# A GNN block on one Trainium2 core: D to the columns of H B H^T by a row through DRAM and a GpSimd product, and another order within a step

## The reference, cut to what matters

```python
def hypergraph_conv(x, adj, W, b):
    H = (adj != 0).astype(x.dtype)
    w = adj.reshape(N, -1)[:, :C]                 # first row of adj
    xw = jnp.einsum('ncd,hd->nch', x, W)
    Dn = jnp.einsum('nce,ne->nc', H, w)
    Dn = jnp.where(Dn > 0, 1.0 / Dn, 0.0)
    Be = H.sum(axis=1)
    Be = jnp.where(Be > 0, 1.0 / Be, 0.0)
    m = Be[:, :, None] * jnp.einsum('nce,nch->neh', H, xw)
    return Dn[:, :, None] * jnp.einsum('nce,neh->nch', H, m) + b
h = layer_norm(relu(hypergraph_conv(x, adj, W1, b1)), gamma, beta)   # 256 -> 512
y = hypergraph_conv(h, adj, W2, b2) + x                             # 512 -> 256
out = _layernorm(x + y)
```

## Time and profile before

| | us |
|---|---|
| runs shown | 300.36, 301.17, 301.25 |
| median | 301.17 |
| the profiled execution | 300.86 |
| its span | 299.1 |
| busy in it: PE | 285.9 |
| DVE | 207.1 |
| ACT | 207.4 |
| POOL | 133.7 |
| q1, SP's queue: share of 16 DMA engines | 23.5% |

### The profile page before, as it was taken

One profiled execution on the slowest core, in us unless ns is written; L12 is line 12 of the kernel. 1 busy time (PEld: TensorE's weight loads), 2 busy tenths in 40 slices (PEclk: granted clock), 3 DMA queues, 4 the chain that ended last, 5 costly groups with the idle time before them and its releaser, 6 DMA issues.

```text
span 299.1 us, 5864 instructions
## 1 busy us (share of the span) xinstructions
PE 285.9 (96%) x1918; PEld 254.5 (85%) x1918; DVE 207.1 (69%) x589; ACT 207.4 (69%) x619; POOL 133.7 (45%) x162
## 2 busy tenths in 40 slices
PE   5799999999999999999999999999999999999972
PEld 5689889798988989898898979898897989988851
DVE  1783686794939587593958669494958759394965
ACT  3498577868687786868677786858778686756430
POOL 2233444617353552636344361735355263636441
PEclk9999999999999999999999999999999999999995
DMA  7921030503114050502305050310304040101112
GB/s 217 297 72 36 1 107 0 175 2 125 56 30 148 0 179 0 172 7 57 120 1 175 2 176 2 109 34 8 133 3 140 2 141 0 59 13 37 37 50 90
DMA packets 26437, 22.55 MB, mean 75 GB/s; under 512 B 860, under 2 KB 26152, under 8 KB 26408
## 3 DMA queue, kind: packets, MB, share of 16 engines
q1 hardware_dynamic: 26304, 22.15, 23.5%
q10 hardware_dynamic: 104, 0.04, 0.0%
HBM read 13.80 MB, written 8.39 MB: 74 GB/s over the span
## 4 chain that ended last, share of the span: by engine, by line
DVE 32%; POOL 27%; issue 23%; PE 11%; ACT 3%; DMA 2%; DVEq 0%; POOLq 0%; SPq 0%
POOL xb_sb L781 11%; DVE r_lo L595 7%; POOL rstd L774 7%; DVE g_sb L586 6%; DVE bn_sb L623 6%; DVE z_sb L615 6%; POOL rstd L796 5%; PE bank_v L253 4%; POOL r_hi L789 4%; DVE mv_sb L633 2%; DMA w_raw<-in_L_gnn_W_dram 2%; PE bank_v L238 1%; POOL shift L801 1%; DVE mean L636 1%; DVE u_lo L558 1%
## 5 line engine op out<-in xcount | busy, mean ns | idle before, releaser
L789 POOL TENSOR_SCALAR r_hi<-r_sb 128x512 fp32r<-128x512 f32 x64 | 48.2, 753 | 82.4 <-ACT r_sb L436 82.4
L261 PE MATMUL bank_g<-w_hi,r_hi 128*128 128x258 f32 x256 | 69.3, 303 | 0.0
L263 PE MATMUL bank_g<-w_lo,r_hi 128*128 128x256 f32 x256 | 63.8, 281 | 0.0
L436 ACT ACTIVATE r_sb<-bank_v,vec 128x512 f32<-128x512 f32 x64 | 44.2, 690 | 15.8 <-PE bank_v L253 15.8
L253 PE MATMUL bank_v<-u_hi,w_hi 128*128 128x512 f32 x128 | 51.9, 406 | 0.4 <-DVE u_lo L558 0.4
L253 PE MATMUL bank_v<-u_lo,w_hi 128*128 128x512 f32 x128 | 50.5, 395 | 0.0
L253 PE MATMUL bank_v<-u_hi,w_lo 128*128 128x512 f32 x128 | 50.4, 394 | 0.0
L263 PEld LDWEIGHTS bank_g<-w_lo,r_hi 128*128 128x128 f32 x256 | 48.4, 189 | 1.0
L261 PEld LDWEIGHTS bank_g<-w_hi,r_hi 128*128 128x128 f32 x256 | 48.3, 189 | 1.1
L595 DVE TENSOR_TENSOR r_lo<-r_sb,r_hi 128x512 fp32r<-128x512 f32 x64 | 47.6, 747 | 1.5 <-POOL r_hi L789 1.5
L268 PE MATMUL bank_g<-w_hi,r_lo 128*128 128x258 f32 x256 | 41.3, 283 | 0.0
(11 more groups left out here) (95 smaller groups left out, 485.2 us busy)
## 6 DMA issues: line engine op xcount, KB each, us to landing
x_sb<-in_x_dram SPq DMA_DIRECT2D x16, 512.0 KB, 3.8
out_dram<-z_sb SPq DMA_DIRECT2D x15, 512.0 KB, 4.6
adj_sb<-in_adj_dram SPq DMA_DIRECT2D x16, 256.0 KB, 5.0
w_raw<-in_L_gnn_W_dram SPq DMA_DIRECT2D x2, 512.0 KB, 6.2
out_dram<-z_sb SPq DMA_DIRECT2D x2, 256.0 KB, 2.2
b_half<-in_L_gnn_b_dram SPq DMA_DIRECT2D x1, 128.0 KB, 7.3
edge_rows<-in_adj_dram ACTq DMA_DIRECT2D x1, 32.0 KB, 3.2
vec_rows<-in_L_gnn_b_dram ACTq DMA_DIRECT2D x1, 2.0 KB
```

Of the source, the lines that this page charges most:

```text
L261: pe.matmul(bank_g[:, n, 0:W2COLS], r_hi[:, i % 2, k, graph(n)], w2_hi[:, k], start=(k == 0), stop=False)
L263: pe.matmul(bank_g[:, n, 0:DOUT], r_hi[:, i % 2, k, graph(n)], w2_lo[:, k], start=False, stop=False, skip_group_check=True)
L436: nc.scalar.activation(r_sb[:, k], bank_v[:, k % 2], ACT.Relu, bias=vec[:, k:k + 1]).then_inc(relu_ready, 1)
L789: nc.gpsimd.tensor_scalar(r_hi[:, i % 2, k], r_sb[:, k], 1.0, 1.0, ALU.mult, ALU.mult).then_inc(r_hi_ready, 1)
```

## The change

S is copied as it is from PSUM to s_sb by ScalarE (read_s), and the degrees with it. make_d works on that copy. SP stores dinv (128 x 4) to a DRAM tensor and loads it back as one row of 512, broadcast to all 128 partitions. GpSimd multiplies S by that row (make_at), which gives A^T. Groups 0 and 1 still go by make_a, turn_a and read_at. The order of a step changes on all engines: TensorE now has g 0, g 1, turn_q, make_u, make_s, g 2, v 0, g 3, v 1, v 2, v 3, y 0, y 1, turn_h(i+4). VectorE has add_squares(i) first, then z of group i-1 before split_u(i+1), make_d(i+2) behind it, then the statistics of z of group i-1, make_h, make_b, make_var1(i) and the rest. GpSimd adds b2 before it splits r, behind a wait for u_lo, and ends a step with make_at(i+2). make_htb(1) goes from ScalarE to GpSimd. The diff without its declarations:

```diff
@@ SP
+            def store_d(j):
+                sp.wait_ge(d_ready, j + 1)
+                sp.dma_start(d_rows[j], dinv[:, j % 2]).then_inc(d_stored, 16)
+
+            def load_d(j):
+                sp.wait_ge(d_stored, 16 * (j - ON_PE + 1))
+                if j >= ON_PE + 2:
+                    sp.wait_ge(at_ready, j - 1)
+                sp.dma_start(d_row[:, j % 2], d_rows[j].rearrange("c n -> (c n)").unsqueeze(0).to_broadcast(
+                    [P, P * PER])).then_inc(d_row_in[j % 2], 16)
             for i in range(G):
                 if i + 6 < G:
                     load_adj(i + 6)
+                if i + 2 < G:
+                    store_d(i + 2)
+                    load_d(i + 2)
                 if i + 3 < G:
                     load_x(i + 3)
-                if i >= 1:
-                    store(i - 1)
+                if i >= 2:
+                    store(i - 2)
@@ TensorE
             def make_s(j):
...
-                if j >= 2:
-                    pe.wait_ge(q_summed, j - 2)
-                else:
-                    pe.wait_ge(a_ready, j)
+                if j:
+                    pe.wait_ge(at_ready, min(j, ON_PE))
+                if j >= ON_PE:
+                    pe.wait_ge(q_summed, j - 1)
+                    if j + 1 < G:
+                        pe.wait_ge(ht_ready, j + 2)
             def turn_q(i):
                 pe.wait_ge(q_ready, i + 1)
-                pe.wait_ge(q_summed, i)
-                pe.wait_ge(a_ready, min(i + 3, G))
+                if i:
+                    pe.wait_ge(q_summed, i)
+                    pe.wait_ge(s_read, min(i, G - ON_PE))
+                else:
+                    pe.wait_ge(at_ready, ON_PE)
@@ TensorE, the loop over i
                 make_g(i, 0)
                 if i == 0:
-                    turn_h(2)
+                    turn_h(3)
+                    pe.wait_ge(c2_ready, 1)
+                make_g(i, 1)
+                if i:
+                    turn_q(i)
                 if not last:
                     make_u(i + 1)
-                if 0 < i and i + 2 < G:
+                if i and i + 2 < G:
                     make_s(i + 2)
+                make_g(i, 2)
                 if i == 0:
-                    pe.wait_ge(c2_ready, 1)
-                make_g(i, 1)
+                    turn_q(0)
+                if not last:
+                    make_v(i + 1, 0)
                 if i == 0:
                     make_s(2)
-                if last:
-                    turn_q(i)
-                else:
-                    make_v(i + 1, 0)
-                make_g(i, 2)
-                if not last:
-                    turn_q(i)
-                if i + 2 < G:
-                    turn_a(i + 2)
                 make_g(i, 3)
                 if last:
                     break
                 make_v(i + 1, 1)
-                if i + 3 < G:
-                    turn_h(i + 3)
                 make_v(i + 1, 2)
                 make_v(i + 1, 3)
                 make_y(i, 0)
                 make_y(i, 1)
+                if i + 4 < G:
+                    turn_h(i + 4)
@@ ScalarE
+            def read_s(j):
+                act.wait_ge(s_made, j + 1)
+                if j > ON_PE:
+                    act.wait_ge(at_ready, j)
+                nc.scalar.activation(s_sb[:, :, :].rearrange("p (b n) e -> p b (n e)", b=2),
+                                     bank_s[:, :, 0:2 * HCOLS], ACT.Copy).then_inc(s_read, 1)
+                if i:
                     sum_q(i)
+                split_u(i + 1)
+                if i == 0:
+                    sum_q(i)
+                if i and i + 2 < G:
+                    read_s(i + 2)
+                if i >= 2:
+                    normalise(i - 2, 0)
+                    normalise(i - 2, 1)
+                relu(i + 1, 0)
+                if i == 0:
+                    read_s(2)
+                for k in range(1, KH):
+                    square(i + 1, k - 1)
+                    relu(i + 1, k)
+                square(i + 1, KH - 1)
@@ VectorE
             def make_d(j):
-                degrees = s_parts[:, :, :, P]
-                dve.wait_ge(s_made, j + 1)
+                if j < ON_PE:
+                    degrees = s_parts[:, :, :, P]
+                    dve.wait_ge(s_made, j + 1)
+                else:
+                    degrees = s_sb[:, :, P]
+                    dve.wait_ge(s_read, j - ON_PE + 1)
...
-                nc.vector.scalar_tensor_tensor(out=dinv[:, :], in0=degrees, scalar=0.0, in1=degree[:, 1],
+                nc.vector.scalar_tensor_tensor(out=dinv[:, j % 2], in0=degrees, scalar=0.0, in1=degree[:, 1],
             for i in range(G):
+                add_squares(i)
+                if i:
+                    make_z(i - 1, 0)
+                    make_z(i - 1, 1)
                 if i < LAST:
                     split_u(i + 1)
                 if i + 2 < G:
                     make_d(i + 2)
-                if i < LAST:
-                    add_squares(i)
+                if i:
+                    take_stats2(i - 1, 0)
+                    take_stats2(i - 1, 1)
+                    make_var2(i - 1)
                 if i == LAST:
                     break
                 if i + 4 < G:
                     make_h(i + 4)
+                if i + 3 < G:
+                    make_b(i + 3)
                 make_var1(i)
                 split_r(i + 1, 0)
                 read_g(i)
                 split_r(i + 1, 1)
...
@@ GpSimd
+            def make_at(j):
+                pool.wait_ge(d_row_in[j % 2], 16 * (j // 2))
+                if j >= 3:
+                    pool.wait_ge(y_made, (j - 2) * 2)
+                nc.gpsimd.tensor_tensor(at_sb[:, j % 3], s_sb[:, :, 0:P],
+                                        d_row[:, j % 2].rearrange("p (c n) -> p n c", n=PER),
+                                        ALU.mult).then_inc(at_ready, 1)
...
+                pool.wait_ge(u_lo_ready, (i + 2) * KD)
+                add_b2(i)
+                split_r(i + 1, 0)
                 if i:
                     inverse_std2(i - 1)
-                if i == LAST:
-                    break
-                split_r(i + 1, 0)
-                add_b2(i)
                 inverse_std1(i)
-                split_r(i + 1, 1)
-                split_r(i + 1, 2)
-                split_r(i + 1, 3)
+                for k in range(1, KH):
+                    split_r(i + 1, k)
+                if i + 2 < G:
+                    make_at(i + 2)
```

More of the change, by code:

```diff
@@ L75, in hypergraph_block @@
         degree = sb("degree", [P, 2, PER])
-        dinv = sb("dinv", [P, PER])
+        dinv = sb("dinv", [P, 2, PER])
+        s_sb = sb("s_sb", [P, PER, HCOLS])
+        d_row = sb("d_row", [P, 2, P * PER])
         a_sb = sb("a_sb", [P, PER, P])
@@ L108, in hypergraph_block @@
         SUM = DOUT
+        d_rows = nc.dram_tensor("d_rows", [G, P, PER], F32, kind="Internal").ap()
+        ON_PE = 2
         weights_in = [sem(f"weights_in{n}") for n in range(4)]
@@ L189, in _ @@
                     load_adj(i + 6)
+                if i + 2 < G:
+                    store_d(i + 2)
+                    load_d(i + 2)
                 if i + 3 < G:
                     load_x(i + 3)
-                if i >= 1:
-                    store(i - 1)
+                if i >= 2:
+                    store(i - 2)
+            store(LAST - 1)
             for half in range(2):
@@ L202, in turn_h @@
                 pe.wait_ge(h_ready, j + 1)
-                if j:
-                    pe.wait_ge(at_ready, j)
+                if j == 1:
+                    pe.wait_ge(at_ready, 1)
+                elif j == 2:
+                    pe.wait_ge(a_ready, 2)
+                elif j == 3:
+                    pe.wait_ge(ht_ready, 3)
+                elif j:
+                    pe.wait_ge(s_read, j - 3)
                 for n in range(PER):
@@ L223, in turn_a @@
                 for n in range(PER):
-                    mm = pe.transpose(bank_h[:, graph(n)], a_sb[:, n], ident[:, :])
+                    mm = pe.transpose(turned_a[j][:, graph(n)], a_sb[:, n], ident[:, :])
                 mm.then_inc(a_turned, 1)
@@ L333, in _ @@
             sum_w2()
+            make_s(1)
             make_v(0, 2)
-            make_s(1)
             make_v(0, 3)
+            turn_a(1)
+            turn_h(2)
             make_c2()
-            turn_a(1)
             pe.wait_ge(w2_ready, 1)
@@ L416, in make_a @@
                     ins = nc.scalar.activation(a_sb[:, n], s_parts[:, n // 2, n % 2, 0:P], ACT.Copy,
-                                               scale=dinv[:, n:n + 1])
+                                               scale=dinv[:, j % 2, n:n + 1])
                 ins.then_inc(a_ready, 1)
@@ L482, in _ @@
             relu(0, 0)
-            make_htb(1)
             relu(0, 1)
+            make_a(1)
             act.wait_ge(w2_centred, 1)
@@ L487, in _ @@
             relu(0, 2)
-            make_a(1)
             relu(0, 3)
             read_at(1)
+            read_ht(2)
```

(15 more changed lines are left out.)

62 lines of the change are left out of this document (21 added, 41 removed).

## The result

The changed kernel takes 325.14 us (median of 4 runs, 324.12 to 325.55), against 300.76 (4 runs, 300.34 to 301.25) for the kernel before beside it: a ratio of 1.080, interval 1.0778 to 1.0821. It is slower, as forecast, but by 24.4 us where 12.5 were forecast, and above the range (298 to 321). The profiled span is 323.7 us.

The account below looks back on a forecast made before the run. TensorE, busy in 96% of the span, was taken as the bound. Thirteen steps of 18.1 instead of 17.14 us add 12.5, group 0 -0.6, group 14 +0.6: 300.86 becomes 313.4, as a median 313.7; range 298 to 321.

Parts of the forecast that it names:

- make_d's last instruction is held: VectorE: with both operands in SBUF, it waits from 3.9 to 5.8 us after make_u's start for GpSimd's b2 addition.
- first sums to GpSimd's rstd 0.91, rstd to g_sb 1.51: First norm on VectorE and GpSimd: these start-to-start times, read from the old profile, put g_sb at 10.8 after make_u's start.
- a product of 1.29: GpSimd's make_at, two inputs of 512 columns: 1.29 us, on a line between additions of 4 and 1024 columns.
- A: The forecast itself: both GpSimd collisions hold VectorE, the product going right behind r_hi(3): 313.7 us, chance 0.40.
- B: VectorE keeps the shared port through back-to-back instructions, so the product waits for the end of q: 307 us, chance 0.20.
- q and turn_q: End of VectorE's step: q ends at 17.4, z at 18.05, and make_u of the next group starts 0.05 later.
- The sum: Whole kernel: 13 steps add 12.5 us, group 0 gains 0.6, group 14 loses 0.6, tail 0, onto 300.86.
- TensorE's saving of 0.59 a step: TensorE without turn_a, one fp32 entry into g and turn_h's switch back: step 16.55 if it never waits, 0.59 less.
- turn_h's part: TensorE: turn_h read as 0.31 us; moved behind y, its four transposes alone are 0.20, so 0.11 is saved.
- The row through DRAM: SP's store of dinv and load of the row: taken as 2.2 + 2.7 us, in time, so nothing charged.
- rival D: The row lands 3 us after the product's place is free; product falls into sums or behind q: 307 to 314, chance 0.08.
- Rival E: Neither collision on VectorE, at make_d and r_lo(1), costs anything, so TensorE runs through: 292.7 us, chance 0.18.

Follow-up runs that it names:

- product cut: Changed kernel with b2's addition back at q, rstd2 ahead of r_hi(0), product on VectorE but only one column a graph computed from group 2 on: 296.77 us, 0.987.
- the last version: Changed kernel, b2's addition at q, product on VectorE, g 2 before turn_q, rstd2 and shift ending GpSimd's step, make_var1 before make_h and make_b: 295.67 us, 0.981.

## Why the prediction was wrong in size

The sign, the kind of mechanism and two of the places were right: TensorE gives up the bound, y waits for g_sb, and q is late behind the product. What failed first is which instruction of make_d is held. The step by the forecast's own points, for group 6 and for group 7, which stands for most:

| from U, us | forecast | group 6 | group 7 |
|---|---|---|---|
| stats begin | 5.7 | 6.24 | 6.21 |
| g_sb begins | 10.8 | 11.46 | 11.43 |
| y begins | 11.75 | 12.39 | 12.37 |
| r_lo(1) begins | 12.4 | 13.04 | 13.01 |
| pair sums begin | 15.5 | 14.84 | 16.18 |
| q has ended | 17.4 | 18.07 | 18.18 |
| next U | 18.1 | 18.82 | 18.93 |

- **"make_d's last instruction is held"** was the step that failed first. It is the first one, and the other two follow only after the addition: stats at 6.21, 0.51 late, 6.6 us over 13 steps and more than half of the miss. The forecast took the rule from rows of two-input instructions and applied it to the only such instruction in make_d. The runs show that a one-input fp32 tensor_scalar from SBUF to SBUF is held as well, even at four columns. The Trainium skill, "SBUF — State Buffer", Who interferes with whom, names VectorE's two-port modes among what contends with GpSimd, beside two-input reads; the traces agree (2.32 for 0.17, mean 0.72, h 0.86). Before the change make_d read PSUM, so its rows could not show this.
- **"first sums to GpSimd's rstd 0.91, rstd to g_sb 1.51"** was taken from the old order. Now rstd1 stands 0.6 us behind rstd2 and shift, and is 0.4 shorter: 0.12 more in all. The 1.40 of the old rstd1 was itself 0.4 of waiting for r_lo(0), a small GpSimd instruction behind a two-input one of VectorE, which the forecast read as its own length.
- **"a product of 1.29"**: 1.56 at the least, 1.18 without the 16-byte steps; the mean as recorded, waiting for the port included, is 2.00. The interpolation by columns was 0.11 too high, the steps cost 0.38 (a third). The forecast had the page's rule ("GPSIMD Engine Reference" of the Trainium skill, Performance pitfalls for Q7 kernels) at half as much again for the columns, and left it to the range; the direction holds, and the size here is 0.38 of 0.98.
- **"served at its first chance"** (A, 0.40) against "waits for the end of q" (B, 0.20): A was right in 11 of the 13 steps, in place and nearly in price. It charged 3.1 us from r_lo(1) to the pair sums; group 7 has 3.17. That it is so near is luck in part: the product costs an r_lo 1.36 where 1.1 was charged, and r_hi(3) doesn't hold r_lo(1), where 0.17 was charged. In groups 6 and 12 it is served ahead of q, short of B's place, and costs 1.23 (sums and q take 3.16 start to start for 1.93). Why it passes several changes of VectorE's instruction there stays open.
- **q and turn_q**: the forecast ended q where h began, 0.08 too early, and let z set the next make_u. It is q's end: turn_q starts 0.06 behind it and takes 0.69 behind an idle stretch (0.44 without). Together 0.15 a step.
- **The sum**: 0.51 and 0.12 up to y, 0.07 at the product and 0.15 at q and turn_q make the 0.83 of group 7, rounding aside; in the mean of the 13 the loss is 1.72 and not 0.96: 9.9 us. Group 14 cost 1.7, not 0.6; group 0 and the start gave nothing where 0.6 were booked, and lost 0.1; the tail cost 0.4: 2.2 more. Together 12.1, the miss between the profiled executions (325.47 against 313.4); between the medians it is 11.4.
- **TensorE's saving of 0.59 a step** was too large. (turn_h's part was read as 0.31 where its rows give 3.09 - 2.76 = 0.33.) The changed order without waits (product cut) takes 16.74, a saving of 0.38, and the last version 16.67, but in another order of TensorE. y was booked at its 1.78 in front of g; in front of turn_h it is 1.97, and the 0.11 that moving turn_h was to save are lost there.
- **The row through DRAM** (rival D) was booked at 4.9 us and left at that. From make_d's end to the product it is 6.5 to 8.0, and 12 of 14 products wait for it, by 0.15 to 1.5 us. It sets which r_lo is held, not how much: steps with the row 0.15 and 1.07 late take 18.93 and 18.95.
- **Rival E** (292.7) had no chance in the changed order, whose own time is 296.8 with the product cut; its mechanism is what the last version gets to, at 295.7.

The miss would have been smaller with two more readings: what a tensor_scalar does when its source moves from PSUM to SBUF, and why the power took 1.40 us in the kernel before.

## What to carry to other kernels

When TensorE is busy in 96% of the span, work taken off it pays only if every loop through the other engines stays shorter than the shortened step; write down each loop (here the first norm to y, and the last r_lo over q to turn_q) before moving work into them, and re-order the work by which loop wants it, which here was worth 14 us of 310: 8.8 by TensorE's order, 5.5 by that of the small operations. In these runs a large GpSimd instruction and a VectorE tensor_scalar from fp32 SBUF to SBUF, or a VectorE instruction with two SBUF inputs, excluded each other: put the large one beside VectorE's PSUM work or gap, and an instruction that was free because it read PSUM can stop being so when its source is copied to SBUF. And read more than one step before a step is called the pattern: here two of 13 looked otherwise.

## What the runs showed of the hardware that was not expected

- A four-column, one-input VectorE tensor_scalar was held 2.3 us by a GpSimd addition of 1024 columns; an r_hi, one-input on GpSimd, was held by a VectorE product (2.23 for 0.62). And two one-input instructions hold each other: h, started 0.04 us behind an r_hi of 0.62, took 0.86 for 0.42. The batch-norm statistics of VectorE, also from SBUF to SBUF, passed beside the addition (four in 1.40, as alone).
- A pending GpSimd product was mostly served between two VectorE instructions that overlap by 0.08 us: at the end of the r_lo in which it became ready, or of the next one, in 11 of 13 steps. In the two others it passed two and three such changes, and was served in a wait of some 0.04 us. What decides stays open.
- 16-byte steps in one of two inputs cost VectorE 0.40 us (1.09 for 0.69) and GpSimd 0.38 (1.56 for 1.18) over 512 columns. "Vector Engine (DVE) Microarchitecture Reference" of the Trainium skill, Measured stream behaviour on trn2, has 1.73 ns a column for one source that hops 4 KiB at each element against 1.05, an estimate of 0.35 us by that page; 16-byte steps are not in its table, and the 0.40 here is near it.
- GpSimd's power of four columns takes 1.00 to 1.02 us by itself. It takes 1.39 when it begins 0.17 us behind an r_lo, and 1.13 when it begins 0.18 behind an h_sb of 0.43: each time it ends 0.87 to 0.88 behind the end of that VectorE instruction. The other way round it held nothing: an r_lo that began 0.07 us behind a power kept its 0.69 (in the version with g 2 first and the product on VectorE).
- Matmuls of y take 1.97 us in front of the four bf16 transposes of turn_h and 1.78 in front of g, start to start.
- TensorE's granted clock was 0.63 in the mean of a stretch of 4 us (so mostly at the lower level, 1.2 GHz), behind one in which it had been busy for 1.56 us, with an idle entry of 2.44; in the next it was at 2.4 GHz again.
